# Pair sums of probability tiles, rotary turn and second high parts on GpSimd, in an adaLN block with attention and a mixture of experts

## The reference, cut to what matters

```python
h = _layernorm(x) * (1 + ca) + sa              # ca, sa, ga, sb, cb, gb from silu(c) @ wmod
q = rope(h @ Wq.T); k = rope(h @ Wk.T); v = h @ Wv.T   # 16 query heads of 32, ONE key/value head
q = rmsnorm(q, w_qn); k = rmsnorm(k, w_kn)             # per head
scores = where(causal, q k^T * 32**-0.5, min); attn = softmax(scores)
x = x + ga * (rmsnorm(attn @ v, w_pre) @ Wo.T)
h = _layernorm(x) * (1 + cb) + sb
x = x + gb * (experts(h) + shared_mlp(h))      # 64 experts, top 8 of 4 of 8 groups, at most 256 rows each
```

## Time and profile before

| | us |
|---|---|
| median of 3 runs (1219.08 to 1219.68) | 1219.67 |
| the profiled execution, its own time | 1219.15 |
| its span, first to last instruction | 1217.4 |
| PE busy in the span | 1161.7 |
| DVE busy | 975.9 |
| ACT busy | 760.7 |
| POOL busy | 493.7 |

### The profile page before, as it was taken

The page is one execution under the profiler, slowest core; times in us unless marked ns, Lnnn a source line. Parts: engine busy times, 40 slices in busy tenths (PEclk is TensorE's granted clock), DMA queues, the critical chain, the costliest instruction groups (busy, mean ns, idle before and its releaser), DMA issues.

```text
span 1217.4 us, 25541 instructions
## 1 busy us (share of the span) xinstructions
PE 1161.7 (95%) x8905; PEld 877.7 (72%) x8905; DVE 975.9 (80%) x1881; ACT 760.7 (62%) x1507; POOL 493.7 (41%) x375
## 2 busy tenths in 40 slices
PE   8988999999999989999998999999999999999996
PEld 4455666555565555565557899999999999999983
DVE  4677787766657889786677889999999999999977
ACT  3456555556665535546754477777777777777741
POOL 1122222111122111111010248888878788778741
PEclk9999999999999989999999999999999999999999
DMA  9480000000000000004003279999999999999988
GB/s 348 152 333 1 1 10 10 10 10 2 15 10 10 10 1 23 1 10 115 23 21 124 84 212 297 302 298 302 295 300 296 298 295 297 301 300 294 299 238 294
DMA packets 75167, 189.95 MB, mean 156 GB/s; under 512 B 11544, under 2 KB 12184, under 8 KB 74832
## 3 DMA queue, kind: packets, MB, share of 16 engines
q1 hardware_dynamic: 44704, 116.27, 28.2%
q0 software_dynamic: 28672, 71.32, 23.7%
q10 hardware_dynamic: 1712, 1.32, 0.3%
HBM read 136.36 MB, written 52.51 MB: 155 GB/s over the span
## 4 chain that ended last, share of the span: by engine, by line
PE 71%; DVE 13%; DVEq 4%; issue 4%; ACT 4%; DMA 2%; POOL 1%; POOLq 0%; SPq 0%; ACTq 0%
PE ps L1349 22%; PE ps L1388 12%; PE ps L1168 8%; PE ps L1335 5%; PE ps L1153 4%; PE ps L1198 4%; PE ps L1113 4%; PE ps L1081 3%; DVE nmax L1631 2%; PE ps L1138 2%; DMA acc_dram<-y,slots 1%; DVEq L1705 1%; PE ps L1216 1%; PE ps L1185 1%; PE ps L1053 1%
## 5 line engine op out<-in xcount | busy, mean ns | idle before, releaser
L751 POOL DMA_INDIRECT acc_dram<-y,slots x128 | 249.6, 1950 | 78.1 <-issue 50.7
L1631 DVE TENSOR_REDUCE nmax<-ps 128x1 f32<-128x512 f32 (+3 forms) x304 | 190.8, 656 | 80.3 <-PE ps L1117 43.0
L860 ACT ACTIVATE probs<-ps 128x512 f32<-128x512 f32 (+1 forms) x320 | 159.0, 555 | 85.5 <-PE ps L1153 82.4
L702 POOL TENSOR_SCALAR_AFFINE_SELECT probs<-probs 128x512 f32<-128x512 f32 x64 | 43.1, 675 | 351.6 <-ACT probs L860 351.6
L736 POOL DMA_INDIRECT xg<-h_dram,slots x128 | 130.4, 1019 | 84.5 <-DVE slots L1822 40.5
L1113 PE MATMUL ps<-kpad,qpT 128*128 128x512 f32 (+3 forms) x384 | 144.5, 444 | 9.9 <-DVE nmax L1631 7.9
L1349 PE MATMUL ps<-x_hi,e_gu_hi 128*112 128x256 f32 (+1 forms) x768 | 120.1, 278 | 0.0
L1349 PE MATMUL ps<-x_hi,e_gu_lo 128*112 128x256 f32 (+1 forms) x768 | 119.6, 278 | 0.0
L1153 PE MATMUL ps<-qT,kT 98*128 98x512 f32 (+1 forms) x320 | 111.8, 428 | 2.6 <-ACT probs L860 1.9
L1349 PEld LDWEIGHTS ps<-x_hi,e_gu_hi 128*112 128x112 f32 (+1 forms) x768 | 105.7, 179 | 5.9
L1349 PE MATMUL ps<-x_lo,e_gu_hi 128*112 128x256 f32 (+1 forms) x768 | 109.9, 279 | 0.0
(11 more groups left out here) (238 smaller groups left out, 2409.1 us busy)
## 6 DMA issues: line engine op xcount, KB each, us to landing
e_gu<-in_gate_up SPq DMA_DIRECT2D x64, 704.0 KB, 7.4
e_d<-in_w_down SPq DMA_DIRECT2D x64, 224.0 KB, 4.7
acc_dram<-h SPq DMA_DIRECT2D x2, 4608.0 KB, 25.8
e_d<-in_w_down SPq DMA_DIRECT2D x64, 128.0 KB, 5.4
wmod_b<-in_wmod SPq DMA_DIRECT2D x2, 2048.0 KB, 23.6
xg<-h_dram SPq DMA_DIRECT2D x16, 256.0 KB, 6.6
acc_a<-acc_dram SPq DMA_DIRECT2D x8, 512.0 KB, 10.9
acc_b<-acc_dram SPq DMA_DIRECT2D x8, 512.0 KB, 6.6
```

The costliest lines, as they stand in the source:

```text
L751: pool.indirect_dma_start(out=acc_dram[a], out_offset=bass.IndirectOffsetOnAxis(ap=slots[:, at:at + 1], axis=0), in_=y[e % 2][:, h, :], in ...
L860: act.activation(probs[:, n % PROBS, 2 * pr:2 * pr + 2, off:CW], unit_bank(2 * n + pr)[:, :, off:CW], ACT.Exp).then_inc(s_exp, 1)
L1631: dve.tensor_reduce(nmax[:, 1 if lo else 0, first:first + heads], max_view(n, heads, hi - lo), AX.X, ALU.max, negate=True).then_inc(s_max, 1)
```

## The change

The product with ones of a pair off the diagonal is replaced: POOL adds the two probability tiles into `p_sum` (two slots), and PE takes ones by that sum, one pair later. Diagonal pairs keep theirs. `rotate` moves from DVE to POOL, where its step with the sum of squares stays on DVE under a new name, `head_squares`; `second_high` moves from ACT to POOL. Calls in the loops change places, some table entries change by 1 to 4, and the scratch of dynamic DMAs is set to 8192 bytes, where the program before leaves it at its default.

```diff
+        p_sum = sb(att, "p_sum", [P, 2, GH, CW])
+        SUM_LAG = 0
-        DIVIDED = [4, 4, 2, 4, 4, 4, 4, 2]
+        DIVIDED = [4, 4, 2, 5, 4, 4, 4, 2]
+        def sums_before(q, g, k):      # sums issued before this one
+            return sum(NG * (keys(i) // 2 - 1) for i in range(q)) + g * (keys(q) // 2 - 1) + k
...
-              ... "squares": -22, "rotate": -14, "head_rms": -11, "split": -9, "second_high": -8, ...
+              ... "squares": -22, "rotate": -16, "head_squares": -13, "head_rms": -11, "split": -9, "second_high": -8, ...
...                                       (entries of MOVED and of the tables of tiles)
@@ gpsimd
+            def rotate(t, n):
+                if n == 0:
+                    pool.wait_ge(s_kve, t + 1)
+                    pool.wait_ge(s_qk, t + 1)
+                    if t:
+                        pool.wait_ge(s_parts, t)
+                    pool.tensor_tensor(t1[:, :, :], qk[:, :, :], cos[...].to_broadcast([P, H + 1, HD]), ALU.mult)
+                elif n == 1:
+                    if t:
+                        pool.wait_ge(s_hi2, t)
+                        pool.wait_ge(s_pack, t)
+                    pool.tensor_tensor(t2[:, :, 0:half], qk[:, :, half:HD], sin[...], ALU.mult)
+                    pool.tensor_tensor(t2[:, :, half:HD], qk[:, :, 0:half], sin[...], ALU.mult).then_inc(s_rope, 1)
+                else:
+                    pool.drain()
+                    pool.tensor_tensor(t1[:, :, :], t1[:, :, :], t2[:, :, :], ALU.add).then_inc(s_turned, 1)
+            def second_high(t):
+                pool.wait_ge(s_t2, t + 1)
+                if t >= 2:
+                    pool.wait_ge(s_st, (t - 1) * NG)
+                pool.tensor_copy(qs[:, t % 2, :, HD:2 * HD].bitcast(f32r), t2[:, 0:H, :]).then_inc(s_hi2, 1)
+            def pair_sum(q, g, k):
+                n, c = step_of(q, g, 2 * k), sums_before(q, g, k)
+                pool.wait_ge(s_exp, 2 * n + 4)
+                if c >= 2:
+                    pool.wait_ge(s_pv, sum_read(c - 2))
+                pool.tensor_tensor(p_sum[:, c % 2, :, :], probs[:, n % PROBS, :, :], probs[:, (n + 1) % PROBS, :, :],
+                                   ALU.add).then_inc(s_psum, 1)
             for m in range(FIRST * H, END):
+                (in this order) causal, rotate (3 places), tile_rstd, head_rms, row_rms, second_high, tiles_rstd,
+                for q, g, kt in steps_at(m, SUM_LAG):
+                    if kt % 2 and kt < keys(q) - CT:
+                        pair_sum(q, g, kt // 2)
@@ scalar: squares, exponentials
+                if t:
+                    act.wait_ge(s_ms, t)
...
                     act.wait_ge(s_pv, (n - PROBS) // 2 + 1)
+                    if kt % 2 == 0:
+                        before = sums_done(n - PROBS + 1)
+                        if before > sums_done(n - PROBS - 1):
+                            act.wait_ge(s_psum, before)
@@ tensor: values
-                for at in (0, CW):
+                for kt in (2 * k, 2 * k + 1):   # v_sb by probs, four heads each, as before
...
+                if k:
+                    c = sums_before(q, g, k - 1)
+                    pe.wait_ge(s_psum, c + 1)
+                    for j in range(GH):
+                        last = pe.matmul(ps[HD * j:HD * j + HD, PV_BANK, CW:2 * CW], ones[:, :], p_sum[:, c % 2, j, :],
+                                         start=False, stop=False)
+                if k == last_pair:              # ones by probs, four heads by two tiles, as before
@@ vector: split
+                    dve.wait_ge(s_turned, t + 1)
-    nc = bacc.Bacc("TRN2", target_bir_lowering=False, num_devices=1)
+    nc = bacc.Bacc("TRN2", target_bir_lowering=False, num_devices=1, dynamic_dma_scratch_size=8192)
```

More of the change, by code:

```diff
@@ L404, in step_of, with sums_done, sum_read @@
             return steps_before(q) + g * keys(q) + kt
+        def sums_before(q, g, k):
+            return sum(NG * (keys(i) // 2 - 1) for i in range(q)) + g * (keys(q) // 2 - 1) + k
+        def sums_done(n):
+            found = 0
+            for q in range(NCHUNK):
+                for g in range(NG):
+                    found += sum(step_of(q, g, 2 * k + 1) <= n for k in range(keys(q) // 2 - 1))
+            return found
+        def sum_read(c):
+            for q in range(NCHUNK):
+                pairs = NG * (keys(q) // 2 - 1)
+                if c < pairs:
+                    g, k = divmod(c, keys(q) // 2 - 1)
+                    return step_of(q, g, 2 * k) // 2 + 2
+                c -= pairs
         def masks_before(q, g, kt):
@@ L486, in build_program @@
[L486 to L492, removed]
@@ L493, in build_program @@
-                 "keys_out": (0, 0, 0, 0, 0, 0, 0, 0, 0, 0, 1, 0, 0, 2, 0, 1),
-                 "end_max": (0, 0, 0, 0, 0, 0, 0, 0, 0, 0, 0, 0, 0, 0, 0, 1),}
+                 "query_out": (-1, 0, 0, 0, 0, 0, 0, 0, 0, 1, 0, 0, 0, 0, 0, -1),
+                 "squares": (0, 1, 0, 0, 0, 0, 0, 0, -1, 0, 0, 0, 0, -1, 0, -1),
+                 "rotate": (0, 2, 0, 0, 0, 0, 0, 0, 0, 0, 0, 0, -1, -1, 0, -1),
+                 "head_squares": (0, 1, -1, 0, 0, 0, 0, 0, 0, -2, 0, 0, 0, 0, 0, 0),
+                 "head_rms": (-1, 2, 0, 0, 0, 0, 0, 0, 0, 0, 1, 0, -1, 2, 0, -1),
@@ L709, in _ @@
             for m in range(FIRST * H, END):
+                for q, g, kt in steps_at(m):
+                    if kt >= keys(q) - CT:
+                        causal(q, g, kt)
+                for tile, n in due(m, "rotate", 3):
+                    rotate(tile, n)
+                for tile, _ in tile_due(m, "rstd"):
+                    tile_rstd(tile)
+                for tile, _ in due(m, "head_rms"):
+                    head_rms(tile)
                 for q in chunk_due(m, "row_rms"):
                     row_rms(q)
+                for tile, _ in due(m, "second_high"):
+                    second_high(tile)
                 for k, at in enumerate(STATS_AT, 2):
@@ L944, in _ @@
                     pack_out(t)
+                for b in range(B):
+                    if m == (NT + 1) * H + 12 + 3 * b:
+                        shared_down_hi(b)
                 for t, _ in due(m, "keys_out"):
@@ L1167, in values @@
                         for j in range(GH):
[L1168 to L1171, removed]
+                            last = pe.matmul(ps[HD * j:HD * j + HD, PV_BANK, CW + off:2 * CW], ones[:, :],
+                                             probs[:, (n + kt % 2) % PROBS, j, off:CW], start=False,
+                                             stop=(kt == keys(q) - 1))
                 last.then_inc(s_pv, 1)
@@ L1303, in _ @@
                     stack(tile, n)
+                for tile, _ in due(m, "turn_x"):
+                    if tile:
+                        turn_x(tile)
                 for tile, n in due(m, "project_q", KC):
@@ L1874, in _ @@
                             hot(tile, part)
+                for tile, _ in tile_due(m, "shift"):
+                    shift(tile)
+                for tile, _ in due(m, "head_squares"):
+                    head_squares(tile)
+                if t == 1 and 9 <= h < 9 + KC:
+                    scale_out(h - 9)
                 for tile, n in tile_due(m, "residual", 2):
                     residual(tile, n)
-                for tile, n in due(m, "rotate", 4):
-                    rotate(tile, n)
                 for b in range(B):
@@ L1883, in _ @@
                         shared_down_lo(b)
-                for tile, _ in tile_due(m, "shift"):
-                    shift(tile)
+                for tile, n in due(m, "split", 4):
+                    split(tile, n)
                 for r in range(NR - 1):
@@ L1897, in _ @@
                     shared_up_lo()
-                for tile, n in due(m, "split", 4):
-                    split(tile, n)
             def rows_lo(n, p):
```

119 lines of the change are left out of this document (48 added, 71 removed).

## The result

The change made the kernel slower: 1254.85 us (median of 4 runs, 1249.26 to 1255.98) against 1219.38 us (4 runs), a ratio of 1.029 (95% interval 1.0271 to 1.0309). The forecast was 1207.5, and the measured time lies above its whole range. The profiled execution took 1255.98 us.

The account below looks back on a forecast made before the run. PE was taken to bound both the chunks and the expert part. From 1219.15: -22.3 (PE's work) + 6 (waits for DVE) + 2 (new waits) + 2 (clock) + 0 = 1206.9 us; forecast 1207.5, range 1200 to 1214.

Parts of the forecast that it names:

- The count of pairs: Products with ones in the chunks: 48 pairs off the diagonal, 384 fewer PE records of 1280.
- The sum's duration: POOL's add of two probability tiles, 128 x 1024: 2.5 us each, 120 us for 48.
- The turn: The rotary turn and high parts on POOL: 4.0 us a tile, 65 us for 16 tiles.
- POOL half full: POOL in the chunks would be busy 270 of 544 us, not a bound by its sum.
- The expert part and the scratch: Smaller scratch of dynamic DMAs, serving only the expert part: 0, bounds 0 and +20 us; slowdown rival 1227, chance 0.05.
- The rival of a late POOL: In the chunks POOL's sums end late and ACT's exp waits: 36 us minus 22.3, 1233 us; chance 0.13.
- DVE pays it back at the memory port: In the chunks POOL's instructions delay DVE by 40 us against 38.8 gained; 6 us more PE waits, bounds -4 and +20.
- The upper bound: Most DVE could lose to POOL at the port: half a sum each time, 48 x 1.25 + 64 x 0.5 = 92 us.
- The third rival: DVE loses 92 us to POOL instead of 40, PE waits about 20 more: 1219 us, no change; chance 0.14.
- The clock: PE with more idle time falls to 1.2 GHz more often: +2 us, bounds -4 and +8.
- PE's relief: In the chunks PE loses 48 x 0.465 = 22.3 us of work on products with ones, counted as -22.3 us.
- Places: Calls moved by 1 to 4 places of 2.11 us: 0, bounds -5 and +5 us.

Follow-up runs that it names:

- small_sum: The changed kernel with POOL's pair sum cut to one element of each partition, waits and places kept: 1204.88 us, 0.9886 of the kernel before.
- pow_sum: The changed kernel with each pair sum replaced by a 13-element power on POOL, about as long: 1202.3 us, 0.9875 of the kernel before.
- no_sums: The changed kernel with the pair sums undone, PE taking ones by both tiles; turn and high parts stay on POOL: 1216.35 us.
- before_turn: The kernel before with only the rotary turn and second high parts moved to POOL, at the old places, no sums: 1214.47 us.

## Why the prediction was wrong

**Held.** The count of pairs and the records saved (384). The sum's duration, 2.5 us taken and 2.38 measured (median). The turn, 4.0 us a tile, measured (22.5 + 22.4 + 14.7 + 12.9)/16 = 4.5. POOL half full (275 of 582 us). The expert part and the scratch at 0. The rival of a late POOL did not come: exp waited 3.7 us for sums.

**The step that failed: "DVE pays it back at the memory port".** The mechanism was right and seen in the rows of before; both its sizes were wrong. First the hold: 40 us taken, 89.3 - 9.1 = 80.2 measured. The rate of 0.1 us per us of POOL came from masks of 0.63 us, and it was low even for them: counted over all forms, the hold in the trace of before is 9.1 us for 43.1 of masks, 0.21. A DVE instruction that arrives waits for the rest of the POOL instruction, so a four times longer one catches more instructions and each for longer: 63.7 us for 116.4 of sums is 0.55, while turn and high parts with the masks stay at 0.2. The upper bound, half a sum for nearly each of them, was the right model (42 caught by 48 sums, 1.5 us each), and I should have taken it.

Second its price: 6 us taken, for "DVE has 10 to 15 us of 32 free". Measured, the hold by sums costs 50 us (changed minus small_sum) to 52.6 (minus pow_sum), 0.8 us per us held. The free time of a window hides what can wait. DVE's queue is in order, its maxima free three PSUM banks for PE, and its division releases L1264. So a good half of the hold went on to PE as idle time: from small_sum to the changed kernel, with 63.7 us of hold by sums more, the idle time that DVE ended rose from 17.0 to 49.9 us. The free share was also read from the best stretches: in the nine stretches of 32 us of before that lie in chunks 2, 3, 6 and 7, DVE has 7.1 to 15.6 us free, and only four have 10 or more. Nor did the loss keep to these chunks: from pow_sum to the changed kernel chunks 1 to 7 grew by 7.2, 7.2, 3.6, 2.2, 8.4, 12.5 and 11.0 us.

**The third rival** named this mechanism and priced it at +20 for 92 us, no change in sum; it was a factor of 2.5 short, by the same error. Its chance was 0.14.

**The clock**, 2 us taken with a bound of 8: 64.9 - 20.5 us more at half clock are up to 22 us of PE's work. It is part of the 50 us and not beside them: it falls where PE stood idle (0.82 from 576 to 608 us with 24.1 us busy of 32, where no stretch of the earlier trace rows is under 0.89). From small_sum to the changed kernel the stretch from 88 us to the last `gram` grows by 48.0 us, of which 33.7 are PE's idle time and 14.3 its busy time for the same work, with 34.2 us more at half clock. That the clock fell because PE was idle was not isolated, since nothing here held the clock up.

**PE's relief**, 22.3 us taken whole; alone it brings 11.5 us, and 14 with pow_sum. In the traces PE's busy time in the chunks falls by 9.8 and 17.4 us against no_sums, and its idle time grows by 4.3 and 5.5.

**Places**, taken at 0 with 5 either way: with the turn on DVE they cost 17.7 us, with it on POOL nothing that shows (no_sums 0.9988 against before_turn 0.9971, with intervals that overlap). The steps from kernel to kernel are +17.7 (places), -19.9 (turn and high parts) and +38.5 (sums: -11.5 relief, +50.0 hold). Their sum, +36.3, must meet the measured difference, since each step starts where the last one ended; it checks nothing. That the first two nearly cancel is luck: the prediction had both at about nothing.

## What to carry to other kernels

An idle GpSimd is not free room: a long add of it on SBUF stops VectorE's instructions with two SBUF inputs, and casts, until it ends. Where VectorE is as busy as here (three quarters of the time), count the hold as half the GpSimd instruction for nearly each one, and price it by who waits behind VectorE's queue, not by VectorE's free share. Test it before with a stand-in that is as long but moves few columns. If the work has to go there, cut it in short instructions and put it only in stages where the other engine's results are not waited for: here that turned +2.9% into -0.9%.

## What the runs showed of the hardware

- A GpSimd add of 1024 fp32 columns takes 2375 ns, of 256 columns 734 ns, of one 191 ns: 2.1 to 2.2 ns a column and some 0.19 us fixed. A power of 13 columns takes 2428 ns and holds VectorE no more than one add of one column does (hold 21.7 and 21.4 us in all).
- VectorE's instruction with one SBUF input and one in PSUM was never held (749 to 753 ns in 16, three of them begun inside a sum), nor was a reduction from PSUM (24 begun inside a sum, none over 692 ns); the same size with two in SBUF took up to 2637 ns for 694. Casts with one SBUF input were held (2460 ns for 428).
- By the Trainium skill (SBUF — State Buffer, "Who interferes with whom") a two-input instruction contends with a GpSimd instruction that reads SBUF and whoever issues first keeps the shared pair for its whole instruction. The adds and masks here agree; the power does not: eleven divisions of two SBUF inputs begun inside a power of 2.4 us took 406 to 426 ns, as they do alone, and there the measurement decides.
- The hold goes both ways: POOL's sum took up to 3665 ns, the quarter up to 2108 for 734. The longest sum began 0.16 us behind a VectorE instruction of 1.62 us and ended 2.2 us, about its own length, after that one's end.
